# Scatter stage: the multiply that weights the extra rows, moved from GpSimd to VectorE

## The reference

```python
for l in range(3):
    f1 = relu(x[row] @ nb_W[l] + nb_b[l]);  f2 = relu(x[col] @ self_W[l] + self_b[l])
    h = relu(concatenate([f1, f2], axis=1) @ att1_W[l] + att1_b[l])
    mask = clip(sigmoid(h @ att2_W[l] + att2_b[l]) * (ZETA - GAMMA) + GAMMA, 0, 1)
    rowsum = segment_sum(mask, row) + 1e-06
    d = clip(rowsum ** -0.5, 0, 10)
    x = segment_sum((mask * d[row] * d[col])[:, None] * x[col], row)
    out = out + x
# then: layer norm; a convolution with weights 1/sqrt(degree) of both ends, @ weight, relu; layer norm
```

## Time and profile before

| | |
|---|---|
| median of 3 runs | 11238.58 us (11231.23 to 11239.19) |
| span of the profiled execution, first to last instruction | 10215.4 us |
| time of the profiled execution itself | not listed; the median lies 1023.2 us above the span |
| TensorE busy | 8439.0 us (83%) |
| VectorE busy | 8039.4 us (79%) |
| GpSimd busy | 4364.3 us (43%) |
| ScalarE busy | 3166.6 us (31%) |
| the moved multiply, 128x128, on GpSimd | 392 times, 156.7 us |

### The profile page before, as it was taken

One profiled execution on the slowest core, in us unless ns is written; L12 is line 12 of the kernel. 1 busy time (PEld: TensorE's weight loads), 2 busy tenths in 40 slices (PEclk: granted clock), 3 DMA queues, 4 the chain that ended last, 5 costly groups with the idle time before them and its releaser, 6 DMA issues. The chain is left out here.

```text
span 10215.4 us, 720231 instructions
## 1 busy us (share of the span) xinstructions
PE 8439.0 (83%) x288671; PEld 7571.9 (74%) x288671; DVE 8039.4 (79%) x13908; ACT 3166.6 (31%) x6110; POOL 4364.3 (43%) x4880
## 2 busy tenths in 40 slices
PE   0113288888887999899997999899997999879996
PEld 0112177877776888799997888799997888768885
DVE  9998488888887777777777777777777777777775
ACT  0110156666663333300002333300001333333332
POOL 0002601111116888311114888521112888758883
PEclk9755599999998999999998999999998999989996
DMA  1001277777765555577775555467775555545552
GB/s 27 0 0 27 49 226 232 230 230 232 229 216 143 162 161 160 142 212 214 211 212 155 161 159 161 130 205 212 212 214 170 161 161 160 141 130 160 159 161 70
DMA packets 1005301, 1633.48 MB, mean 160 GB/s; under 512 B 260439, under 2 KB 743635, under 8 KB 1004831
## 3 DMA queue, kind: packets, MB, share of 16 engines
q1 hardware_dynamic: 954104, 1581.29, 52.8%
q0 software_dynamic: 51104, 50.97, 2.3%
HBM read 1345.54 MB, written 286.24 MB: 160 GB/s over the span
## 5 line engine op out<-in xcount | busy, mean ns | idle before, releaser
L1034 PE MATMUL bank<-tab,extra 128*64 128x64 bf16 x201684 | 3981.3, 197 | 389.0 <-DMA extra<-one_hots 230.4
L1034 PEld LDWEIGHTS bank<-tab,extra 128*64 128x64 fp8e4 x201684 | 3566.3, 112 | 877.4 <-issue 817.2
L739 POOL TENSOR_TENSOR planes<-planes 128x448 f32<-128x448 f32 (+1 forms) x2744 | 2610.2, 963 | 542.5 <-DVE planes L1767 476.1
L888 ACT CAST bank<-planes 128x448 f32<-128x448 bf16 (+1 forms) x2744 | 1515.1, 552 | 2289.5 <-DVE planes L1760 2283.0
L1142 PE MATMUL bank<-planes,extra 128*128 128x192 bf16 x19992 | 2098.2, 247 | 43.1 <-POOL planes L739 10.0
L669 POOL DMA_INDIRECT xg<-q_table,ixb x588 | 561.1, 954 | 3592.0 <-ACT ixb L837 3486.3
L1760 DVE TENSOR_TENSOR planes<-bank,mask_all 128x448 f32<-128x448 f32 (+2 forms) x2744 | 1699.0, 619 | 274.2 <-PE bank L1034 171.0
L1767 DVE TENSOR_TENSOR planes<-planes,bank 128x448 f32<-128x448 f32 (+1 forms) x2744 | 1727.4, 630 | 126.5 <-ACT bank L888 126.4
L1142 PEld LDWEIGHTS bank<-planes,extra 128*128 128x128 fp8e4 x19992 | 1584.2, 96 | 172.7 <-issue 55.0
L1640 DVE SCALAR_TENSOR_TENSOR extra<-bank,a2w 128x448 f32<-128x448 f32 (+1 forms) x2058 | 1300.2, 640 | 510.2 <-PE bank L1059 453.7
L1059 PE MATMUL bank<-plb,extra 128*128 128x64 bf16 x44982 | 1595.9, 194 | 14.4 <-ACT plb L869 9.0
(11 more groups left out here) (227 smaller groups left out, 4734.3 us busy)
## 6 DMA issues: line engine op xcount, KB each, us to landing
extra<-one_hots SPq DMA_DIRECT2D x1372, 368.0 KB, 3.3
extra<-one_hots SPq DMA_DIRECT2D x2156, 224.0 KB, 3.6
extra<-one_hots SPq DMA_DIRECT2D x588, 192.0 KB, 2.4
one_hots<-extra SPq DMA_DIRECT2D x490, 224.0 KB, 2.3
one_hots<-extra SPq DMA_DIRECT2D x294, 368.0 KB, 3.9
work<-slot_rows_cols SPq DMA_DIRECT2D x196, 368.0 KB, 5.2
work<-slot_rows_cols SPq DMA_DIRECT2D x294, 224.0 KB, 4.0
work<-slot_rows_cols SPq DMA_DIRECT2D x98, 192.0 KB
```

Source lines behind the costliest of these rows:

```text
L739: nc.gpsimd.tensor_tensor(tiles(yrl[:, 2, a * C:b * C]), tiles(yrl[:, 1, a * C:b * C]), upper[:, 1, a:b, :], ALU.subtract).then_inc(low_re ...
L888: nc.scalar.copy(tiles(z_banks[g][:, 0:(b - a) * C]), upper[:, 0, a:b, :]).then_inc(high_ps, 1)
L1034: mm = pe.matmul(bank[half * S:(half + 1) * S, i * C:(i + 1) * C], oct_[:, k * P + half * S:k * P + (half + 1) * S], tab[:, at:at + C], st ...
```

## The change

GpSimd's `extra_rows` and its call ahead of low(4) are taken out. VectorE's `weighted` gets, for the last group, the same multiply with the same operands, behind the main rows' one and behind a wait for the gathers. The wait for `sc_ps` is the one that `weighted` of the last group already has. `y_extra` is counted by VectorE, and ScalarE waits for it as before.

```diff
--- before.py
+++ after.py
@@ -720,20 +720,10 @@
 
             def low_planes(t0, layer):
 
-                def extra_rows(t, m, R):
-
-                    wait_alone(pool, xg_in, t * (16 * XT) + 16 * XT)
-                    wait_alone(pool, sc_ps, m * NG + NG)
-                    nc.gpsimd.tensor_tensor(tiles(yrl[:, 0, MT * C:]), tiles(xg[:]),
-                                            mask_all[:, bass.ds(R * TT + MT, XT)].unsqueeze(2).to_broadcast([P, XT, C]),
-                                            ALU.mult).then_inc(y_extra, 1)
-
                 def block_of_rows(t, m, R, late):
                     for g, ts in enumerate(GROUPS):
                         if g < XT:
                             gather_extra(t, g, xd_d)
-                        if g == 4:
-                            extra_rows(t, m, R)
                         a, b = ts[0], ts[-1] + 1
                         wait_alone(pool, z_used, t * NG + g + 1 + NG)
                         nc.gpsimd.tensor_tensor(tiles(yrl[:, 2, a * C:b * C]), tiles(yrl[:, 1, a * C:b * C]), upper[:, 1, a:b, :],
@@ -1760,6 +1750,11 @@
                     v.tensor_tensor(tiles(yrl[:, 0, a * C:at * C]), tiles(z_banks[g][:, 0:(at - a) * C]),
                                     mask_all[:, bass.ds(R * TT + a, at - a)].unsqueeze(2).to_broadcast([P, at - a, C]),
                                     ALU.mult).then_inc(y_ready, 1)
+                    if g == NG - 1:
+                        wait_alone(dve, xg_in, t * (16 * XT) + 16 * XT)
+                        v.tensor_tensor(tiles(yrl[:, 0, MT * C:]), tiles(xg[:]),
+                                        mask_all[:, bass.ds(R * TT + MT, XT)].unsqueeze(2).to_broadcast([P, XT, C]),
+                                        ALU.mult).then_inc(y_extra, 1)
 
                 def rest(m, g):
                     a, b = CUTS[g], CUTS[g + 1]
```

## The result

The changed kernel takes 11318.23 us in the median of 4 runs (11314.16 to 11323.75). The kernel before, run beside it, takes 11235.73 (11231.23 to 11239.19). The ratio is 1.0074, 95% interval 1.0059 to 1.0088: 82.5 us slower, where no change was forecast.

What follows compares the result with a forecast made beforehand. TensorE was taken as the bound, with the delay absorbed in each block: span 10215.4 + 2.7 = 10218.1 us, plus 1023.2 outside it, gives 11241.3 us, no change (chance 0.76); range 11222 to 11275.

Steps and rivals of the forecast that it cites:

- Removed from GpSimd ... gain: nothing.: GpSimd between low(3) and low(4): dropping the 0.40 us multiply brings low(4) forward 0.18 us, which nobody waits for.
- I take it to be held till low(4) ends ... shows about 0.88 us.: VectorE's new multiply waits for GpSimd's low(4), showing 0.88 us instead of 0.29 and making VectorE 0.80 us late.
- VectorE stands ready 0.94 us before sums: End of the block on VectorE: slack before `sums` shrinks from 1.48 us to 0.94 but still absorbs the delay.
- The rival with low(5): Hold makes low(5) late for TensorE's 14 matmuls: up to 113 us slower, 56 with half the excess; chance 0.15.
- Second gather 3515.53 ... everything is caught up within the block: 0 us in each of some 97 blocks.: GpSimd's second gather starts at 3515.53 instead of 3514.99, low(1) stays on time, and each block loses 0 us.
- the forecast's own sign of being wrong: Scatter-stage block: prediction is wrong if the 10.56 us period moves by over 0.05 us.
- The median lies 1023.2 us above that span, which the edit does not touch.: Whole kernel: timed median 11238.58 minus profiled span 10215.4 us, treated as a fixed part added to the forecast.
- 34 us, a third of its 113: Upper end of the range: the hold costs TensorE 34 us, called a third of the rival's 113, giving 11275.
- The end of a stage, 2.7 us: Last scatter of each stage waits for low(6), 0.68 us late; 2.7 us over four stages.

Runs made afterwards that it cites:

- e4: The kernel before with GpSimd's extra-row multiply left out and nothing in its place, waits and count kept, on chip A: 10224.32 us, ratio 1.000.
- e6: The changed kernel with the VectorE multiply reading one input from PSUM instead of the gathered rows, on the other chips: 11258.16 us, ratio 1.0021.
- e2: The changed kernel, unchanged, run again with a profile on chip A: 10312.53 us, ratio 1.0088.
- e9: The kernel before with a 448-column GpSimd multiply (0.93 us) added ahead of each block's first gather in the scatter stages: 11454.76 us, ratio 1.0197.
- e12: The kernel before with both gathers of each scatter block replaced by GpSimd multiplies of the same length: 10964.88 us, ratio 0.976.
- e19: The changed kernel with only each scatter block's second gather left, the first replaced by an equally long GpSimd multiply: 11418.18 us, ratio 1.0067.
- e11: The changed kernel with both gathers of each scatter block replaced by GpSimd multiplies of the same length: 10983.79 us, ratio 0.9778.
- e1: The kernel before, unchanged, run again with a profile on chip A: 10223.17 us, ratio 1.0000.
- e5: The kernel before with one more 128x128 GpSimd multiply ahead of each block's first gather in the scatter stages, on the other chips: 11242.69 us, ratio 1.0004.
- e3: The kernel before with the VectorE multiply added into an unread scratch tile, GpSimd keeping its own, on chip A: 10266.19 us, ratio 1.0043.
- e13: The changed kernel with the next block's first gather ahead of low(6), its indices copied after rest(5), on the other chips: 11197.08 us, ratio 0.9965.

## Why the prediction was wrong, step by step

- *"Removed from GpSimd ... gain: nothing."* Right: e4, 1.000.
- *"I take it to be held till low(4) ends ... shows about 0.88 us."* Right in kind, near in size: 0.81 in the median on chip A (0.58 on the other chips), 0.28 where nothing holds it (e6). The Trainium skill (SBUF — State Buffer, "Who interferes with whom") has the rule that two SBUF inputs on VectorE contend with a reading GpSimd. What was missing in front, a tensor_tensor that shows it, is in e2, and with e6 as its counterpart the runs agree with the rule.
- *"VectorE stands ready 0.94 us before sums"*, low(5), low(6) and low(1) in time: right. It is 0.98 us in the timeline, and TensorE waits for a low plane no more than before. The rival with low(5) is out, although its price, 56 to 113 us, happens to hold the measured size. Its mechanism didn't occur.
- *"Second gather 3515.53 ... everything is caught up within the block: 0 us in each of some 97 blocks."* This step failed. The forecast saw that the second gather would start 0.54 us later, and priced only its landing, for VectorE's wait, and GpSimd's time to low(1). Nothing waited for the landing. It had no term for what a gather's start does to TensorE. On chip A that start stood 0.12 us behind the start of TensorE's run of 84 matmuls before and 0.62 after. The run then took 1.69 us instead of 1.52 and the scatter behind it came late, 0.22 us a block net, which met the forecast's own sign of being wrong (over 0.05 us). Times 388 blocks that is 85 us, where 82.5 and 89.3 were measured; the 40 quick blocks don't pay it, and the two spans differ by 78. On the other chips e6, e9 to e12 and e19 tie the loss to the gathers. There the place is another. The second gather starts 0.18 us behind the run's start, and part of the 0.2 us a block comes behind the first gather.
- Behind that step stood a way of reading: it took each wait of a semaphore as the only tie between engines. The place had no row in the profile of before, because with the gathers where they stood TensorE had 0.0 us of idle time before its small matmuls in 3300 to 4000 us. A resource that isn't short yet leaves no row.
- *"The median lies 1023.2 us above that span, which the edit does not touch."* Wrong as an account: a span and its time are under 2 us apart, and the rest lies between executions on two chips. It did not spoil the sign, since the loss is about the same on both, but it hid that on the other chips TensorE's small matmuls have 658 us of "issue" idle (changed kernel), where on chip A the kernel before has 61.5. Of these, 202 and 7 lie in the scatter stages.
- *"34 us, a third of its 113"*, which set the upper end of the range: a third is 38. The measured time lies beyond either.
- *The end of a stage, 2.7 us*: too small to be told apart from the rest.

What stays open: by what path a GpSimd gather holds TensorE up. That it runs short of instructions there is a reading of "issue"; the profile shows the pause and its place and names no releaser. It is also open why on chip A a gather at 0.62 us costs and one at 0.12 or 0.82 doesn't, and what makes the chips differ; each was measured at one time only, so chip and hour aren't told apart. The 16 us between e11 and e12 outside the scatter stages have no explanation either. All that stands outside the stages takes 6805 to 6829 us in the traces from the other chips but that of e19, without a pattern.

## What to carry to other kernels

When an edit moves the start of a software-driven DMA, even inside slack and even with a landing that nobody waits for, ask what TensorE is doing about 1 us after that start, and treat "issue" idle time inside or behind long runs of small matmuls as a possible tie between the two. Compare a span only with the time of its own execution; if they differ by more than a few us, they come from different executions. Where gathers share a block with dense matmuls, their place in GpSimd's program order is a tuning knob of its own: here it was worth -0.35% to +3%, and must be measured.

## What the hardware showed that was not expected

- Taking two gathers a block out of the scatter stages, in GpSimd time replaced one for one, made the kernel before 273 us (2.4%) faster on the other chips, though no engine waited for them. Its four scatter stages then take 4152 us, what they take on chip A with the gathers (4157, e1). The Trainium skill (SBUF — State Buffer, "Who interferes with whom") says that DMA never contends with a compute engine; that is about SBUF's ports. TensorE's loss here has no semaphore and no port in its rows, only "issue", and is there all the same.
- The kernel before took 10223 us on one chip, 11237 to 11244 on four others and 11343 on a sixth, each steady within 0.3%. A block of the scatter stage ran at 10.56 us on the first; on the others blocks of the changed kernel ran at 11.5, and at 10.5 to 12.1 as the gathers were moved. Most of the difference lies outside the scatter stages. All that stands outside them takes 6067 us in e1, 6807 in e5 and 6918 on the sixth chip (e19).
- The hold works both ways. Where VectorE's multiply got in first (e3's quick blocks, 0.28 us), GpSimd's low(4) behind it took 1.06 us instead of 0.93.
- A stage can lock into one of several periods and change over in mid-stage, with the same instructions in each block. In its first stage e3 went from 10.6 to 10.8 us and e2 from 10.8 to 10.57. In e13 blocks of 12.1 and 10.5 us took turns.
